# A two-layer decoder in fp32 on one core: routed experts for the chosen token pairs only, and another order of work in its slot attention

## The reference

```python
probs = jax.nn.softmax(h @ w_router, axis=-1)             # 8 experts
top_w, top_i = jax.lax.top_k(probs, 2)                    # ffn1 also divides top_w by its sum
combine = jnp.sum(one_hot(top_i, 8) * top_w[..., None], axis=1)
g = jnp.einsum('th,ehi->eti', h, w_gate_e)                # 8 experts, 256 -> 176
u = jnp.einsum('th,ehi->eti', h, w_up_e)
y = jnp.einsum('eti,eih->eth', jax.nn.silu(g) * u, w_down_e)
routed = jnp.einsum('eth,te->th', y, combine)
sh = jax.nn.silu(h @ w_sh_gate) * (h @ w_sh_up) @ w_sh_down   # 704 wide in ffn0, 352 in ffn1
sh = sh * jax.nn.sigmoid(h @ w_sh_eg)                         # ffn0 only
x = x + routed + sh
```

## Time and profile before

| | us |
|---|---|
| median of 3 runs | 7270.35 |
| the runs | 7265.84, 7287.19, 7270.35 |
| the profiled execution's own time | 7269.92 |
| its span in the trace | 7268.1 |
| PE busy | 6523.9 (90%) |
| DVE busy | 4568.6 (63%) |
| ACT busy | 3877.4 (53%) |
| POOL busy | 1427.7 (20%) |

### The profile page before, as it was taken

One profiled execution on the slowest core, in us unless ns is written; L12 is line 12 of the kernel. 1 busy time (PEld: TensorE's weight loads), 2 busy tenths in 40 slices (PEclk: granted clock), 3 DMA queues, 4 the chain that ended last, 5 costly groups with the idle time before them and its releaser, 6 DMA issues. The chain is left out here.

```text
span 7268.1 us, 125259 instructions
## 1 busy us (share of the span) xinstructions
PE 6523.9 (90%) x46184; PEld 4842.4 (67%) x46184; DVE 4568.6 (63%) x9293; ACT 3877.4 (53%) x8283; POOL 1427.7 (20%) x1721
## 2 busy tenths in 40 slices
PE   8999999999999999999999997878899989788999
PEld 5776777767676676767767676756555556576555
DVE  5777777777777777777777775667322257665222
ACT  5767667666676767666676674446211134343111
POOL 2222222223232222222222232311000000010000
PEclk9999999999999999999999998889899999998999
DMA  1000000000000000000000000010111100101111
GB/s 34 5 2 6 5 2 6 5 2 6 6 1 6 6 1 6 6 4 3 6 5 2 6 1 28 11 47 2 33 37 39 32 14 2 48 15 24 45 52 36
DMA packets 64396, 107.61 MB, mean 15 GB/s; under 512 B 12080, under 2 KB 35184, under 8 KB 62832
## 3 DMA queue, kind: packets, MB, share of 16 engines
q1 hardware_dynamic: 63728, 98.86, 4.4%
HBM read 94.34 MB, written 4.49 MB: 14 GB/s over the span
## 5 line engine op out<-in xcount | busy, mean ns | idle before, releaser
L131 ACT ACTIVATE ffn0b_sl<-PSA 128x512 f32<-128x512 f32 x136 | 81.2, 597 | 619.1 <-PE PSA L63 619.1
L131 ACT ACTIVATE ffn1b_sl<-PSA 128x512 f32<-128x512 f32 x112 | 66.9, 597 | 508.5 <-PE PSA L63 508.5
L72 PEld LDWEIGHTS PSA<-E0D,ffn0b_hidden 128*128 128x128 f32 x1088 | 206.7, 190 | 85.3 <-issue 64.1
L63 PE MATMUL PSA<-H0T,E0G 128*128 128x512 f32 x544 | 257.4, 596 | 3.0 <-DVE ffn0b_hidden L107 3.0
L95 DVE TENSOR_TENSOR ffn0b_up<-PSA,ffn0b_CB 128x512 f32<-128x512 f32 x88 | 60.8, 691 | 316.1 <-PE PSA L63 303.6
L95 DVE TENSOR_TENSOR ffn1b_up<-PSA,ffn1b_CB 128x512 f32<-128x512 f32 x88 | 60.9, 692 | 314.6 <-PE PSA L63 303.5
L72 PE MATMUL PSA<-E0D,ffn0b_hidden 128*128 128x256 f32 x1088 | 256.7, 379 | 0.0
L63 PE MATMUL PSA<-H0T,E0U 128*128 128x512 f32 x544 | 255.7, 592 | 0.0
L1216 ACT ACTIVATE gsa_caa<-PSA,gsa_nmxa 128x128 f32<-128x128 f32 x256 | 90.6, 366 | 294.9 <-DVE gsa_nmxa L1013 294.9
L1145 ACT ACTIVATE gsa_cab<-PSA,gsa_nmxb 128x128 f32<-128x128 f32 x256 | 90.6, 366 | 280.1 <-DVE gsa_nmxb L878 280.1
L1301 POOL TENSOR_TENSOR gsa_ssa<-gsa_ssa,gsa_neghalf 128x4 f32<-128x4 f32 x64 | 88.1, 1377 | 732.7 <-DVE gsa_ssa L925 732.7
(11 more groups left out here) (676 smaller groups left out, 20021.6 us busy)
## 6 DMA issues: line engine op xcount, KB each, us to landing
gsa_wa<-in_w_heads SPq DMA_DIRECT2D x16, 512.0 KB
...
```

The source lines that it names most:

```text
L63: last = nc.tensor.matmul(bank[:, :], w[:, c, k * 128:(k + 1) * 128], HT[:, c, g * 512:(g + 1) * 512], start=(c == 0), stop=(c == 1))
L72: last = nc.tensor.matmul(PS[4 + j][:, 0:256], hidden[step % HIDDEN][:, j * 128:(j + 1) * 128], WD[:, k, :], start=(k == 0), stop=(k == ch ...
L131: nc.scalar.activation(sl[step % 2][:, :], PS[step % 2][:, :], ACT.Silu).then_inc(silu_by_act, 1)
```

## The change

There are three parts.

**Experts.** Only the shared expert's chunks still run over all tokens: 48 steps in `ffn0b`, 24 in `ffn1b`. The routing moves from the end of `ffn0a` and `cross` into `moe`, on DVE between the products of the first steps, and goes on: two matmuls (`count`) and DVE give each of the 8192 pairs a place in `PAIRS`, a DRAM array of rows sorted by expert and padded so that each 128 rows have one expert. POOL scatters the normalized rows there, 64 indirect DMAs of 128 rows of 1088 bytes (a row and its mark, its number). After `lead` groups of the shared expert (4 in `ffn0b`, so 24 steps; 5 in `ffn1b`, so 15) come 71 tiles of 128 rows: SP loads one from an offset in a register, PE turns it, multiplies it by the weights of the expert that a register names (two matmuls of 352 columns), turns the product and multiplies it by the down weights (two of 256), and POOL scatters the result to `RESULTS` by the marks (71 indirect DMAs of 128 rows of 1 KB). The rest of the shared expert's steps follow (24 and 9), while SP loads the results (16 x 512 KB) and DVE adds each to X, times its weight. The weights, 2.9 MB (`WGU`) and 2.1 MB (`WD`), are loaded at the start of `moe`, no longer in the stage before.

**Blanks.** `PAIRS` of both blocks is filled with blank rows first, by 16 DMAs from DRAM to DRAM that ACT issues at the end of `prep` (4.7 MB each, 75.8 MB in all; `order` prints each as 34x4x8704 elements). POOL waits for them in `moe`, before its first scatter.

**Slot attention.** The same work is written in another order, and three of the six AM products of each half move from DVE to POOL (`reach_a_by_pool`, `reach_b_by_pool`).

The core of the diff in `moe` and `prep`:

```diff
+                probabilities()
+                for step in range(LEAD):
                     product(step)
+                    if step == 0:
+                        first_choice()
+                        second_choice()
+                    if step == 1:
+                        keep_counts()
+                    if step == 2:
+                        ranks()
+                    if step == 3:
+                        table()
+                    if step == 4:
+                        weights()
                     if step % chunks == 1 and step >= chunks:
-                        add(step // chunks - 1)
-                add(GROUPS - 1)
+                        add(step // chunks - 1, 0)
+                add(lead - 1, 0)
...
+                pe.wait_ge(table_by_dve, 9)
...
+                which = {}
+                for s in range(-2, TILES + 1):
+                    if s + 2 < TILES and (s + 2) % BATCH == 0:
+                        first = s + 2
+                        _, values = nc.values_load_multi_w_load_instructions(TAB[0:1, 1, first:first + BATCH], engines=[mybir.EngineType.PE], min_val=0, max_val=7, skip_runtime_bounds_check_because="a count of seven comparisons")
+                        for k in range(BATCH):
+                            which[first + k] = values[k]
+                    if 0 <= s + 2 < TILES:
+                        turn_rows(s + 2)
+                    if 0 <= s + 1 < TILES:
+                        widen_rows(s + 1, which[s + 1])
+                    if 0 <= s < TILES:
+                        turn_inner(s)
+                    if 0 <= s - 1 < TILES:
+                        narrow_rows(s - 1, which[s - 1])
...
+                def widen_rows(t, e):
+                    pe.wait_ge(xturned_by_act, t + 1)
+                    if t >= 2:
+                        pe.wait_ge(inner_by_dve, t - 1)
+                    for c in range(2):
+                        last = nc.tensor.matmul(PS[2 + t % 2][:, 0:352], xT[t % 2][:, c, :], WGU[:, c, bass.ds(e, 1), :].rearrange("p o f -> p (o f)"), start=(c == 0), stop=(c == 1))
+                    last.then_inc(widened_by_pe, 1)
...
+                def narrow_rows(t, e):
+                    pe.wait_ge(iturned_by_dve, t + 1)
+                    if t >= 2:
+                        pe.wait_ge(result_by_act, t - 1)
+                    for c in range(2):
+                        last = nc.tensor.matmul(PS[6 + t % 2][:, 0:256], hT[t % 2][:, c, :], WD[:, bass.ds(e, 1), c, :].rearrange("p o d -> p (o d)"), start=(c == 0), stop=(c == 1))
+                    last.then_inc(narrowed_by_pe, 1)
...
+                def index(t):
+                    dve.wait_ge(rows_in[t % ROWS], 16 * (t // ROWS + 1))
+                    if t >= IS:
+                        dve.wait_ge(result_out[(t - IS) % YS], 16 * ((t - IS) // YS + 1))
+                    nc.vector.tensor_copy(XI[t % IS][:, :], XS[t % ROWS][:, 256:257]).then_inc(index_by_dve, 1)
...
+                def silu_rows(t):
+                    act.wait_ge(widened_by_pe, t + 1)
+                    if t >= 2:
+                        act.wait_ge(inner_by_dve, t - 1)
+                    nc.scalar.activation(sg[t % 2][:, :], PS[2 + t % 2][:, 0:176], ACT.Silu).then_inc(gated_by_act, 1)
+                def result_up(t):
+                    act.wait_ge(narrowed_by_pe, t + 1)
+                    if t >= YS:
+                        act.wait_ge(result_out[t % YS], 16 * (t // YS))
+                    nc.scalar.activation(Y[t % YS][:, :], PS[6 + t % 2][:, 0:256], ACT.Copy).then_inc(result_by_act, 1)
...
+                def scatter(k, i, done):
+                    nc.gpsimd.indirect_dma_start(PAIRS[:, :], bass.IndirectOffsetOnAxis(ap=POS[:, k, i:i + 1], axis=0), HK[:, i, :], None).then_inc(done, 16)
+                pool.wait_ge(marked, 16)
+                pool.wait_ge(blanked, 128)
+                pool.wait_ge(rank_by_dve, 11)
+                for half in range(2):
+                    for i in range(16 * half, 16 * half + 16):
+                        scatter(0, i, scattered[half])
+                for half in range(2):
+                    pool.wait_ge(scattered[half], 256)
+                    marks = HK[:, 16 * half:16 * half + 16, 256]
+                    nc.gpsimd.tensor_scalar(marks, marks, 4096.0, None, ALU.add).then_inc(remarked_by_pool, 1)
+                    pool.wait_ge(remarked_by_pool, half + 1)
+                    for i in range(16 * half, 16 * half + 16):
+                        scatter(1, i, scattered[2])
+                for t in range(TILES):
+                    pool.wait_ge(index_by_dve, t + 1)
+                    pool.wait_ge(result_by_act, t + 1)
+                    nc.gpsimd.indirect_dma_start(RESULTS[:, :], bass.IndirectOffsetOnAxis(ap=XI[t % IS][:, :], axis=0), Y[t % YS][:, :], None, bounds_check=8191, oob_is_err=False).then_inc(result_out[t % YS], 16)
...
+                nc.sync.dma_start(CONST[:, :], io[prefix + "_const"]).then_inc(loads, 16)
+                nc.sync.dma_start(WGU[:, :, :, :], io[prefix + "_wide"]).then_inc(experts_in, 16)
+                nc.sync.dma_start(WD[:, :, :, :], io[prefix + "_down"]).then_inc(experts_in, 16)
+                sp.wait_ge(table_by_dve, 9)
+                sp.wait_ge(scattered[0], 256)
+                sp.wait_ge(scattered[1], 256)
+                sp.wait_ge(scattered[2], 512)
+                for t in range(TILES):
+                    if t % BATCH == 0:
+                        _, begins = nc.values_load_multi_w_load_instructions(TAB[0:1, 0, t:t + BATCH], engines=[mybir.EngineType.SP], min_val=0, max_val=SLOTS - 128, skip_runtime_bounds_check_because="a sum of counts that the shapes bound")
+                    if t >= ROWS:
+                        sp.wait_ge(xturned_by_pe, t - ROWS + 1)
+                        sp.wait_ge(index_by_dve, t - ROWS + 1)
+                    nc.sync.dma_start(XS[t % ROWS][:, :], PAIRS[bass.ds(begins[t % BATCH], 128), :]).then_inc(rows_in[t % ROWS], 16)
+                for k in range(YS):
+                    sp.wait_ge(result_out[k], 16 * len(range(k, TILES, YS)))
+                sp.wait_ge(narrowed_by_pe, TILES)
+                for g in range(GROUPS):
+                    if g >= 4:
+                        sp.wait_ge(combined_by_dve, 2 * (g - 3))
+                    for k in range(2):
+                        first = 4096 * k + 512 * g
+                        nc.sync.dma_start(zbank(g)[:, k, :, :], RESULTS[first:first + 512, :].rearrange("(i p) d -> p i d", p=128)).then_inc(results_in[g % 4], 16)
...
+                for pairs, blanked in blanks:
+                    for part in range(8):
+                        nc.scalar.dma_start(pairs[part * 4352:(part + 1) * 4352, :].rearrange("(b p) d -> b p d", p=128), io["blank"].unsqueeze(0).to_broadcast([34, 128, 272])).then_inc(blanked, 16)
```

One stretch of PE's order in `gsa` (the other half, and the other engines, change alike):

```diff
-                        pe.wait_ge(softmax_b_by_act, m * 2 + 1)
-                        for j in range(4):
-                            last = nc.tensor.transpose(tile(PS[5], j), tile(CAb[:, :], j), IDENT[:, :])
+                        pe.wait_ge(level_b_by_dve, m * 12 + 12)
+                        for j in range(4):
+                            last = nc.tensor.transpose(tile(PS[4], j), tile(QKb[:, 0:512], j), IDENT[:, :])
                         last.then_inc(softmax_b_by_pe, 1)
                     if within:
                         if gp == 0:
@@ -582,24 +967,30 @@
                         if before:
                             pe.wait_ge(residual_a_by_dve, (n - 1) * 1 + 1)
                         for c in range(2):
-                            last = nc.tensor.matmul(PS[2][:, :], WA[:, c, 0 * 128:1 * 128], XT[:, c, gp * 1024 + 0:gp * 1024 + 0 + 512], start=(c == 0), stop=(c == 1))
+                            last = nc.tensor.matmul(PS[3][:, :], WA[:, c, 1 * 128:2 * 128], XT[:, c, gp * 1024 + 0:gp * 1024 + 0 + 512], start=(c == 0), stop=(c == 1))
                         last.then_inc(projected_a_by_pe, 1)
                         if gp == 0:
                             pe.wait_ge(proj_weights_dma, h * 16 + 16)
                         for c in range(2):
-                            last = nc.tensor.matmul(PS[3][:, :], WA[:, c, 1 * 128:2 * 128], XT[:, c, gp * 1024 + 0:gp * 1024 + 0 + 512], start=(c == 0), stop=(c == 1))
+                            last = nc.tensor.matmul(PS[2][:, :], WA[:, c, 0 * 128:1 * 128], XT[:, c, gp * 1024 + 0:gp * 1024 + 0 + 512], start=(c == 0), stop=(c == 1))
                         last.then_inc(projected_a_by_pe, 1)
+                    if before:
...
+                        nc.gpsimd.tensor_tensor(blocks(AMb[:, 0, :], 2), righttiles(AAb[:, :, 0:128], 2), rightblocks(Yb[:, 0, 0:512], 2), ALU.mult).then_inc(reach_b_by_pool, 1)
```

1192 lines of the change are left out of this document (667 added, 525 removed).

## The result

The changed kernel takes 7918.68 us (median; 7905.48 to 7929.21), the kernel before, measured beside it, 7275.27: a ratio of 1.0883, 95% interval 1.0858 to 1.0907. It is slower by 643 us, where 437 us of gain were forecast. The profiled execution's span is 7920.9 us, 652.8 more than before's 7268.1.

The account below looks back on a forecast made before the run. PE work was taken to bound the expert blocks, and short waits, so order, to count in gsa. -226 - 193 - 10 + 7 + 15 - 30 = -437 takes 7270 to 6835 us; own range 6740 to 6930, wider 6700 to 7055.

Parts of the forecast that it names:

- +15, bounds 0 and 230: Start of gsa: blank copies delay its first load and first heads' weights by 15 us; 230 if ACT were held.
- among the rivals, at 0.03: End of prep: ACT is held while two engines write the blanks at 20.6 GB/s each, 1840 us, total 8660; chance 0.03.
- -226 said: First expert block: 139 us lead, 223 for 71 tiles, 124 for other steps, 8 for last add; 494 instead of 720.
- -193 said: Second expert block: 92 us lead, 37 waiting for scatters, 223 tiles, 46 for nine steps, 8 at end; 406 instead of 599.
- -30 said: gsa: half of PE's 0.49 us wait before the slots product goes, 0.23 us in each of 128 halves.
- -10 said: cross: its 23.41 us wait for a context load shortens by some 10 us, with 0.9 MB instead of 5.4 ahead.
- +7 said: End of prep: ACT issues 16 more DMAs at 0.35 to 0.43 us each before gsa can start, about 7 us.
- serial tiles: Expert blocks: tiles run in series at 6.4 us instead of 3.0, 483 us more, total 7318; chance 0.05.
- scatter at 3 us: Expert blocks: POOL's issue of a scatter costs 3 us; 91 and 102 us more, total 7030; chance 0.12.
- loss in gsa: gsa: the new order costs 1 us a half, total 6993; chance 0.08.
- the rival that gains 1 us a half: gsa: the new order gains 1 us a half, total 6737; chance 0.12.
- the fall to 0.81: Expert tiles: PE's clock granted at 0.81 would make 2.5 us 3.1, at most 85 us more.

Follow-up runs that it names:

- run 9: Changed kernel with SP issuing blanks in gsa, a 16-block copy per array after each head's weights (two after the first's), instead of ACT in prep: 6640.65 us, ratio 0.9141.
- run 1: Changed kernel with the blanks as 8 copies of 68 blocks instead of 16 copies of 34: 7320.57 us, ratio 1.0068 to the kernel before.
- run 2: Changed kernel with the blanks as one copy of 272 blocks for each array: 6812.58 us, ratio 0.9369 to the kernel before.
- run 3: Changed kernel with the blanks as 34 copies of 16 blocks, 17 for each array: 6947.38 us, ratio 0.9555 to the kernel before.
- run 11: Run 9's kernel with copies of 17 blocks, one a head for each array: 6730.75 us, ratio 0.9259 to the kernel before.
- run 6: Kernel before with only the function gsa of the changed one: 7192.64 us, ratio 0.9896 to the kernel before.
- run 7: Run 9's kernel with gsa of before in all but SP's part with the blanks: 6721.44 us, ratio 0.9242 to the kernel before.

## Why the prediction was wrong

**The step that failed: Blanks, "+15, bounds 0 and 230".** It asked when POOL needs the blanks (5100 us later: right) and took it that ACT is free as soon as it has issued them. For the rest it had two rows that don't bear on it: 330 GB/s from loads that had all 16 engines (DMA share 0.97 to 1.03 from 4758 to 4773 us), and that SP was not held by three large loads. Measured: +1271.5 us, 1226 of them until SP may issue gsa's first weights (L1752, at 1292.85 instead of 67.2), ACT held by its own issues, and 46 because these weights land while blanks are still in flight (51.6 to the first matmul instead of 5.8; in run 9, with the blanks issued behind them, 5.3). The sign named for it, gsa's first matmul later than 95 us, is what the profile shows. The mechanism stood among the rivals, at 0.03, with 1840 us; it was sized with two engines, a number that no row of before shows and the changed kernel's DMA share does (0.13 of 16), with 20.6 GB/s for each, where one moved 27, and as if ACT had to wait for all of the blanks, where it was free with two copies still to go. What should have raised its chance was in the text already: 16 copies one behind another on an engine on which a barrier waits. How many of the 16 engines a copy used was measured only afterwards, by the DMA share: two with 34 blocks (0.13, changed kernel), four with 68 (0.25, run 1), all 16 with 272 (0.99, run 2) and with 16 (1.00, run 3), one with 17 (0.07, run 11). Each of these numbers divides its number of blocks; other sizes were not run.

**Without that hold** the change is worth 7273 - 6641 = 632 us (run 9), where the other terms said 452 (437 and the 15 of the blanks).

- *First expert block*, -226 said, -281.5 measured. The tiles were mis-sized: 3.0 us taken, 2.49 measured, the lower bound; 36 of the 55 us. From the first tile to the first matmul of the tail is 180 us, not 220, so another 4 lie in filling and draining. The lead took 131.6, not 139: beyond its 24 steps it took 8 us, where 15 were taken for the start and the routing. The 3 us for the first rows did not come, and what follows the tiles is 5 us shorter.
- *Second*, -193 said, -258.2 measured. 36 us are the tiles again. The scatter, 1.4 taken, is 1.27, and its start is 23 us into the block, not 29: the tiles start at 109.5, not at 132 (129 and 3 for the first rows), and the wait that was named at 37 us is 27.
- *gsa*, -30 said, 73 to 81 measured (runs 6, 7). The key-query product comes 15.4 us after the half's start (3005.54 to 3020.98), not 14.9: the waits before it are 2.2 us, not 3.0, and PE's work before it 13.2, not 11.9. The wait ahead of the slots product, of which half was to go, is gone. But the mechanism was right only in part: the prediction counted waits and put PE's busy time at no change ("Same instructions"), and that fell by 75 us (run 6), for a reason that stays open. The range of 128 us either way held the result.
- *cross*, -10 said: the wait for the context fell only from 23.4 to 18.1 us (L3309), and infini and cross together from 800.4 to 796.9.
- *prep*, +7 said: no run tests it, since in run 9 the copies are not in prep (gsa starts at 72.4). At 0.63 us for an issue that is not held, 16 would be 10 us, an estimate.
- *mlstm and ffn0a* take 734 to 751 us from run to run; nothing is to be read from the -7.8.
- *Rivals*: no serial tiles, no scatter at 3 us, no loss in gsa; its 98 us in run 6's trace, 0.76 a half, are nearer to the rival that gains 1 us a half than to the 0.23 of the sum. PE's clock in the tiles was granted at 0.98 and 0.99, so the fall to 0.81 did not come.
